# A cross-attention and quantised FFN kernel: one block from the projections to the attention's output, with the maxima of two head groups taken in the projections

## The reference

```
q, k, v = layernorm(x) @ Wq + bq, ctx @ Wk + bk, ctx @ Wv + bv
x = x + softmax(q k^T / sqrt(32), masked) v @ Wo + bo
      # image rows (768) see their own third of the image; text rows (256) see
      # all image tokens and, causally, the text
xn = layernorm(x)
xq = fake_quant(xn)                  # int8 grid, scale from the largest |xn| of all
h  = silu(xq @ Q(w_gate)^T) * (xq @ Q(w_up)^T)      # I = 1408
x = x + fake_quant(h) @ Q(w_down)^T  # Q: int8 grid, one scale per row
```

## Time and profile before

| | |
|---|---|
| three runs | 1151.24, 1147.26, 1150.76 us; median 1150.76 |
| the profiled execution | 1151.39 us, span 1149.6 us, mean granted clock 0.951 |
| busy share of the span | PE 92%, PEld 62%, DVE 66%, ACT 44%, POOL 56% |
| DMA | 223.86 MB, mean 195 GB/s |

### The profile page before, as it was taken

How to read it: one execution, slowest core, us unless ns; L and a number is a source line. 1 busy time by engine, 2 the same in 40 slices (tenths; PEclk the granted TensorE clock), 3 DMA queues, 4 the chain that set the end, 5 groups by cost and what they waited for, 6 DMA issues and landing times. The chain is left out here.

```text
span 1149.6 us, 18244 instructions
## 1 busy us (share of the span) xinstructions
PE 1056.8 (92%) x6550; PEld 707.7 (62%) x6550; DVE 754.6 (66%) x1351; ACT 511.3 (44%) x882; POOL 639.0 (56%) x347
## 2 busy tenths in 40 slices
PE   5999999999629999999999999899986799999898
PEld 4888888888516656656666666457865344444343
DVE  5665456654329667776777777335988487777785
ACT  3322223222102667666776666671111455554553
POOL 3434454344440889998999999754764112100373
PEclk9999999999955999999999999799998799999899
DMA  5987677856699897898999863348996454100876
GB/s 201 322 259 236 218 279 257 270 172 196 208 178 194 172 228 166 196 201 184 205 208 209 200 154 122 98 129 226 327 255 226 119 200 148 36 1 1 326 241 220
DMA packets 134324, 223.86 MB, mean 195 GB/s; under 512 B 29672, under 2 KB 60136, under 8 KB 132778
## 3 DMA queue, kind: packets, MB, share of 16 engines
q1 hardware_dynamic: 134250, 222.89, 70.1%
HBM read 137.65 MB, written 80.62 MB: 190 GB/s over the span
## 5 line engine op out<-in xcount | busy, mean ns | idle before, releaser
L800 ACT ACTIVATE a_probs<-a_banks 128x512 f32<-128x512 f32 (+2 forms) x512 | 233.4, 535 | 135.4 <-PE a_banks L1016 101.4
L733 POOL TENSOR_TENSOR a_pair_sums<-a_probs,a_probs 128x2048 f32<-128x2048 f32 x48 | 221.7, 4620 | 69.8 <-ACT a_probs L800 61.1
L875 DVE TENSOR_REDUCE a_max<-a_banks 128x2 f32<-128x512 f32 x192 | 123.0, 684 | 53.6 <-PE a_banks L987 53.4
L1016 PE MATMUL a_banks<-a_queries,a_keys 97*128 97x512 f32 x384 | 147.6, 428 | 8.4 <-ACT a_probs L800 6.3
L992 PE MATMUL a_banks<-a_keys,a_queries 96*128 96x512 f32 (+1 forms) x256 | 115.1, 463 | 2.7 <-DVE a_max_parts L875 2.7
L987 PE MATMUL a_banks<-a_keys,a_queries 96*128 96x256 f32 x384 | 86.2, 319 | 32.2 <-DMA a_queries<-q_split 32.1
L871 DVE CUSTOM_DVE_ANT_0 a_masked_scores<-a_banks,kept_mask 128x384 f32<-128x384 f32 (+1 forms) x128 | 79.5, 621 | 46.5 <-PE a_banks L992 46.3
L875 DVE TENSOR_REDUCE a_max_parts<-a_banks 128x1 f32<-128x512 f32 x128 | 87.8, 686 | 26.1 <-PE a_banks L992 22.7
L987 PEld LDWEIGHTS a_banks<-a_keys,a_queries 96*128 96x128 f32 x384 | 69.8, 204 | 54.9 <-DMA a_queries<-q_split 32.8
L1389 POOL TENSOR_TENSOR d_out<-d_out,f_x 128x512 f32<-128x512 f32 x28 | 42.6, 1551 | 96.5 <-DVE d_out L1417 96.5
L225 POOL TENSOR_SCALAR p_x<-p_x,p_neg_mean,p_rstd 128x512 f32<-128x512 f32 x32 | 28.1, 889 | 121.6 <-DVE p_rstd L330 121.6
(11 more groups left out here) (173 smaller groups left out, 2208.6 us busy)
## 6 DMA issues: line engine op xcount, KB each, us to landing
a_keys<-k_split SPq DMA_DIRECT2D x48, 512.0 KB, 8.1
a_queries<-q_split SPq DMA_DIRECT2D x48, 512.0 KB, 14.3
f_x<-x_scratch SPq DMA_DIRECT2D x14, 1024.0 KB, 7.8
p_c<-in_ctx_dram SPq DMA_DIRECT2D x8, 1024.0 KB, 8.8
p_x<-in_x_dram SPq DMA_DIRECT2D x8, 1024.0 KB, 11.0
v_scratch<-p_v_stage SPq DMA_DIRECT2D x16, 512.0 KB, 9.1
k_split<-p_stage_hi SPq DMA_DIRECT2D x16, 512.0 KB, 4.2
k_split<-p_stage_lo SPq DMA_DIRECT2D x16, 512.0 KB, 5.3
```

Of the source, the lines that this page charges most:

```text
L733: pool.tensor_tensor(PP[u % 2], PR[2 * c % 4], PR[(2 * c + 1) % 4], ALU.add).then_inc(paired, 1)
L800: act.activation(PR[kt % 4][:, j, 0:w], STB[:, n % NST, 0:w], ACT.Exp, scale=SCALE).then_inc(edone, 1)
L875: dve.tensor_reduce(out, src, AX.X, ALU.max).then_inc(wfree, 1)
L1016: op = pe.matmul(out.rearrange("p (c t) -> p c t", t=SIT), keys, q, start=True, stop=True)
```

## The change

The projections and the attention with its output become one block, and share one set of 8 PSUM banks and the two arenas of SBUF.

- **Banks and buffers of the projections.** Items go round banks 0, 1, 2, 6, 7 (`NB = 5`), the attention's three banks of pieces are apart. Two stage pairs serve k and then q. Context, turned context and turned x have one buffer instead of two. `FR` is a buffer of its own.
- **Order in a step.** On VectorE the layernorm of the next chunk moves from between x and k to among q (`moments` behind its first tile, `deviations` behind its third), and `ffn_rows` from among k to behind q's third and fourth tile (first and second in the last step). SP stores the FFN rows behind the next step's v stores, and loads the next ones behind the first k store.
- **Maxima of groups 0 and 1.** Stack 0 is loaded in steps 4 and 5, stack 1 in steps 5 and 6. The 28 pieces of group 0 are put behind q's tiles of step 5 (2 each), v's and q's of step 6 (4 and 1 each), those of group 1 behind v's and q's of step 7 (4 and 3 each). The turn and shift row of group 0 come in step 7.
- **First groups.** The pieces of groups 2, 3 and 4 are spread over 7 slots each from slot 3 of group 0 on. `TURN_SLOT` is 3. Stack 2 is loaded behind the last q store, shift row 1 ahead of stack 3. The last FFN store lies in group 0, the scales' in group 1.
- **Output stage.** `root(n)` ahead of `hi(n + 2)`, `lo(n + 1)` behind the first tile of `chunk(n)`.

The core of the diff:

```diff
+NB = 5
+EARLY = 4
-TURN_SLOT = 1
+TURN_SLOT = 3
+CATCH_UP, SHORT = 3, 7
...
+        STG = [tuple(mem.over(f"p_stage_{part}{i}", (4 + i) * TILE + h * TILE // 2, [P, 2, CH], F32R)
+                     for h, part in enumerate(("hi", "lo"))) for i in range(2)]
+        PB = (0, 1, 2, 6, 7)
         def bank(u, i):
-            return BK[:, (KT + u * ITEMS + i) % NB, :]
+            return BK[:, PB[(KT + u * ITEMS + i) % NB], :]
...
+            def step(b, u):
+                n = 2 * b + u
+                late = n - EARLY if isinstance(n, int) else None
+                last = not more(n, 1)
...
                 for i in range(2):
+                    A.load_early(sp, late, i)
+                if more(n, 2):
                     s.reach(sp, free, NB + at(n) + XTURN + KT)
                     load_x(n + 2, u)
+                stage_store(n, 0)
+                s.reach(sp, fst, 32 * (n + 1))
+                ffn_load(n, u, b)
+                stage_store(n, 1)
+                A.load_early(sp, late, 2)
...
+                if more(n, 2):
+                    s.reach(sp, free, NB + at(n) + CTURN + KT)
+                    load_c(n + 2)
+                if late == 2:
+                    sp.wait_ge(full, at(n) + CTURN + KT)
+                    for part in range(3):
+                        A.load_stack(sp, 1, part)
+                stage_store(n, 2)
+                A.load_early(sp, late, 3)
+                stage_store(n, 3)
+                if not last:
+                    for i in range(2):
+                        value_store(n + 1, i)
+                        if i == 0 and not more(n, 2):
+                            A.shift_rows(sp, 0)
+                    ffn_store(b, u)
...
             def staged(u, n, i, j, use, bias):
                 if j % 2 == 0:
-                    act.wait_ge(sout[stage + j // 2], 32 * (n + 1))
+                    act.wait_ge(sout[j // 2], 32 * (2 * n + use + 1))
...
                 for j in range(KT):
+                    staged(u, n, query(n) + j, j, 0, (3 if more(n, 1) else 2) * KT + j)
+                    if more(n, 1) and j == 0:
+                        moments(1 - u, n + 2, b + u)
+                    if more(n, 1) and j == 2:
+                        deviations(1 - u, n + 2)
+                    if more(n, 1) and j >= 2:
+                        ffn_rows(n, j - 2)
+                    elif not more(n, 1) and j < 2:
+                        ffn_rows(n, j)
+                    if j == (3 if more(n, 1) else 1):
+                        ffn_rows(n, 2)
+                        ffn_rows(n, 3)
+                    for i, k in A.early(n, KT + j):
+                        A.largest(dve, i, k)
...
+        FIRST = [(n, item) for n, items in ((EARLY + 1, range(KT, 2 * KT)), (EARLY + 2, range(2 * KT)), (EARLY + 3, range(2 * KT)))
+                 for item in items]
+        COUNT = (2,) * 4 + (4,) * 4 + (1,) * 4 + (4,) * 4 + (3,) * 4
...
             for i in range(NGRP):
                 if i == 0:
+                    load_values(sp, 1)
+                    for row in range(6):
+                        load_stack(sp, 2, row)
+                    front.ffn_last(sp)
                 store(i, 0)
                 if i > G and i % G == 1:
                     store_recs(i // G - 1)
+                if i + 1 < NGRP:
+                    shift_rows(sp, i + 1)
                 store(i, 1)
+                if i == 0:
+                    for row in range(6):
+                        load_stack(sp, 3, row)
...
+                if u < 2:
+                    pool.wait_ge(front.sout[u], 32 * (2 * NCH + 1))
...
             for n in range(NCH):
+                root(n)
                 if n + 2 < NCH:
                     hi(n + 2)
-                root(n)
...
                     op = dve.bn_stats(ST[:, t, :], X1[u][:, t, :])
+                    if t == 0 and n and n + 1 < NCH:
+                        lo(n + 1)
...
-                if n + 2 < NCH:
-                    lo(n + 2)
```

More of the change, by code:

```diff
@@ L362, in step @@
                     dve.wait_ge(full, at(n) + VALUE + t + 1)
-                    dve.tensor_tensor(VST[t // 2][:, t % 2, :], bank(u, VALUE + t), BV[:], ALU.add).then_inc(free, 1)
+                    dve.tensor_tensor(VST[t // 2][:, t % 2, :], bank(u, VALUE + t), BV, ALU.add).then_inc(free, 1)
+                    for i, k in A.early(n, t):
+                        A.largest(dve, i, k)
+                    if t == 0 and not more(n, 1):
+                        A.rows_out(dve, 0)
                 for j in range(KT):
-                    turned(XT[u], u, n, XTURN + j, j)
@@ L381, in _ @@
             weight(0, "v")
-            layernorm(0, 1, 0)
+            moments(0, 1, 0)
+            deviations(0, 1)
             weight(1, "k")
@@ new lines, in load_early, with sync @@
+        def load_early(sp, late, place):
+            part = 4 * late + place if late is not None else 9
+            if part < 6:
+                load_stack(sp, 0, part)
+            elif part < 9:
+                load_stack(sp, 1, part - 3)
+        A.load_early = load_early
+        A.load_stack, A.load_values, A.shift_rows, A.ones_row, A.early = load_stack, load_values, shift_rows, ones_row, early
+        A.wfree, A.pieces, A.reduced, A.masked = wfree, 0, 0, 0
+        def sync(sp, front):
@@ L1029, in values @@
                     pe.wait_ge(ifree, 3 * i + kt // 2)
+                if kt == 0 and i == 0:
+                    for bank in (6, 7):
+                        pe.wait_ge(front.free, front.cleared(bank))
                 if kt == 0:
@@ L1112, in _ @@
                 pe.wait_ge(olo, m + 1)
[L1113 removed]
+                chunk(m)
+        A.tensor = tensor
+        return A
 class Scale:
```

661 lines of the change are left out of this document (351 added, 310 removed).

## The result

The changed kernel takes **1191.3 us** (median of 4 runs, 1188.4 to 1197.9), the kernel before beside it 1149.0 (1146.7 to 1151.2): ratio 1.039, 95% interval 1.036 to 1.043. It is 42 us slower. The forecast was 1134 with a range that ended at 1152; even the slower rival (B, 1159) is 32 us short of it.

What follows compares the result with a forecast made beforehand. Projections were held bound by TensorE, the attention by GpSimd, so its chain's start counts. Pair sums 10 us earlier, first groups 2 us lost, output stage 9 gained: -17 us, 1134 us; eight in ten 1117 to 1152.

Steps and rivals of the forecast that it cites:

- B: Rival: the ring reaches TensorE in every projection step, rounds over 40 us, half clock after long stalls; 1159 us, chance 0.10.
- The ring: Projections: q's staging waits for k's store behind FFN load, FFN store and quantising; round 37.4 to 39 us, 14 us reach TensorE.
- The 7 us of slack: Projections: the ring can fall back about 7 us before it reaches TensorE, as the norm is wanted at the next x turns.
- Pieces: Projections, steps 5 to 7: maxima of groups 0 and 1 add 15 us of TensorE and 17.5 us of VectorE's backlog.
- Seam at the end of the projections: GpSimd's first pair sum starts 7.8 us after the projections' end, at 361.2, 10 us earlier than before.
- Groups 0 to 3: First attention groups: late stack 2 and group 2's shift row cost 2 us (0 to 6), GpSimd's slack taking most.
- Output stage: With the root first, VectorE's wait goes and chunks take 12.5 us; 9 us gained, range 2 to 11.
- A: Rival: the DMA queue keeps up in the projections and the ring's 14 us vanish; 1120 us, chance 0.22.
- C: Rival: the output stage stays with the DMA queue, 7 us more than forecast; 1141 us, chance 0.13.
- D: Rival: the shift row is late in each steady attention group, about 10 us in all; 1144 us, chance 0.10.

Runs made afterwards that it cites:

- experiment 4: Changed kernel with the maxima of groups 0 and 1 behind the projections, block and early stack rows as changed: 1190.4 us.
- experiment 12: 11 without the edit of (10), with that of experiment 4, and stack 3 behind group 0's shift row: 1123.6 us, ratio 0.981 to the kernel before.
- kernel of 8: Experiment 3's kernel with x ahead of FFN store, that between late v stores, early stack rows behind q's stores, stack 4 behind a shift row: 1157.5 us.
- (10): Kernel of 8 with the pieces of the maxima put behind k tiles instead of q tiles: 1150.5 us.
- Experiment 3: Changed kernel with the norm's deviations and both FFN row maxima at q's second tile instead of its third and fourth: 1165.8 us.
- experiment 6: Kernel of Experiment 3 with each step's x load issued ahead of the FFN store instead of behind it: 1159.4 us.
- experiment 2: Changed kernel with the next context load moved from behind k's second store to behind q's last one: 1193.0 us.
- experiment 1: Kernel before with only the change's output stage (root ahead of hi(n+2), lo(n+1) inside chunk n): 1143.1 us, ratio 0.996.
- 11: Kernel of 8 with the edits of experiment 9 and (10), without that of experiments 5, stack 3 directly behind the first output store: 1146.1 us, ratio 0.997.
- experiments 5: Changed kernel with the six rows of stack 4 issued behind group 2's shift row instead of ahead of it: 1192.1 us.
- experiment 9: Changed kernel with the shift rows of groups 1 to 15 issued on ScalarE's queue instead of SP's: 1181.6 us.

## Why the prediction was wrong

The end of the projections in five kernels separates the two causes:

| last projection matmul done at | maxima behind | maxima inside |
|---|---|---|
| transfers ordered as in the change | 351.0 (4) | 388.5 (the change) |
| ring opened | 309.0 (12) | 351.2 (8), 341.8 (10) |

The numbers in brackets are those of the experiments. "Opened" means the transfers reordered and the row maxima at q's second tile. The kernel before ends the projections at 306.8. So the ring costs 37 us with the pieces inside and 42 without them, and the pieces 37.5 us with the ring and 33 to 42 without it: the two add up to within 5 us. By way of (4), 42.0 for the ring, 37.5 for the pieces and the 2.2 between 306.8 and 309.0 make the 81.7.

**The ring: right mechanism, the step that failed is its size.** The prediction named it (k store, FFN load, FFN store, quantising) and put a round at 37.4 to 39 us; it is 42.3 to 43.6. The part on the engines was right: from the landing of k's second store to the FFN store 21.3 us measured, 0.95 + 2.2 + 0.7 + 1.9 + 13.6 + 1.6 = 21.0 foreseen. The DMA part was 16 to 17, and is 21.7 (77.36 to 99.09): FFN store, x, two k pairs and FFN load, issued within 8 us, are 4.8 MB, and in this burst they move at 4.8/21.7, some 220 GB/s (the queue's whole rate in this stretch is 263, with what is issued behind them), where I gave the 1 MB transfers 380. The prediction wrote that B decides from a round of 40 us and is worth 28 us; it took 14 as the "middle of 0 and 21". At 42 to 43 us it is 6 a step in steps 2 and 3, and 10 in step 4, where the first stack rows go out: 24 us at the x turn of step 5 (236.48 less 211.60, of which 0.9 is the start), and with the steps behind it 42 to 44 in all (experiment 4). Experiment 3 shows it by moving one link, experiment 6 by taking 1 MB out, experiment 2 that the load behind has no part in it. The 7 us of slack held for one step and a half.

**The clock behind a wait: put at nothing.** The forecast counted waits, and only rival B spoke of half clock. Counted in the timelines up to the end of the projections, 82 of the 1110 512-column projection matmuls of the changed kernel start 0.43 us apart instead of 0.23 or lie between the two, 58 in experiment 4, 52 in the kernel of 8, and 15 before the change as in experiment 12. The time added is some 8 us of the ring's 42 (experiment 4 against 12) and 6 to 7 of the pieces' cost. TensorE's waits are another 28 us of the ring's 42; the remaining 6 were not traced.

**Pieces: the sum was short.** 32.5 us forecast (15 of TensorE, 17.5 of waits); 37.5 measured with the changed order, 42.2 with the ring opened. The sum of the waits is right, by luck: TensorE waits 17.3 us for reductions in the kernel of 8, 11.2 behind q tiles, where 6.6 were foreseen, and 6.1 behind v tiles, where 10.2 were. Behind a q tile VectorE, from which TensorE wants a piece bank back, is itself waiting, in order, for the low part of the tile and so for a k store's landing; I had walked VectorE's own work and left out what it waits for. The trace of before could not show it, since no such pair stood there. What was missing in the sum are 1.6 us of waits for stack rows (6.6 in the changed kernel) and the slow matmuls behind the waits: 15 + 17.3 + 1.6 + 6.7 are 40.6 of the 42.2. The 15 are the forecast's own estimate and were not measured apart. With pieces at k tiles the 32.8 us look like the forecast's, but they hold 7.8 of waits for rows.

**Seam at the end of the projections: right.** The first pair sum was put 7.8 us behind the end; it is 7.7 (388.5 to 396.1), by quantising.

**Groups 0 to 3: wrong by 19 us.** Forecast +2 (0 to 6), measured +21.5 (from +24.9 to +46.4), the second largest miss. Both waits were named: stack 2 landed 24 us behind the end (21 foreseen) and cost 5.6 us at slot 3; the shift row of group 2 was "wanted 5 us before it lands" and cost 13.4: SP, held for 11.4 us by one store, issued it 8 us late, and it took 10.5 us to land between the stacks. I took issues as free. "GpSimd's slack takes most" was a hope; GpSimd has hardly any gap in a steady group. Before, stacks 0 and 1 were issued ahead of the first scores and stack 2 at 356.6, 15 us ahead of the first pair sum; stacks 3 and 4 followed at 380 and 390; the change issues stack 2 at 392, 4 us ahead of it, and 3 and 4 back to back from 419 to 433.

**Output stage: right, smaller.** Forecast 9 (range 2 to 11); 5.7 by the trace, 4.4 (1.7 to 7.0) by the timed comparison. The wait for the root is gone as foreseen; the term that failed is 12.5 us a chunk to the end, since the last two chunks take 15.0 and 14.5 (experiment 1).

**Rivals.** A (the queue keeps up) is refuted: ScalarE waits for k's stores in each of steps 1 to 6. C gave the output stage 2 us and the forecast 9; the 4.4 to 5.7 measured lie between them. D is refuted: the landing's median fell to 3.0 us. B is what happened (steps 2 and 3 take TensorE 42 us), and the time is 32 us above its price; the largest parts are 14 to 16 us in the ring (42 to 44 instead of 28), 15 in the first groups and 5 in the pieces. The chance of slower, 0.10, was far too low: ring, stacks and shift row leaned on one queue, and I added them as if they were independent.

**What the change itself is worth.** Its output stage, the one block and the early stacks, with the shift rows on ScalarE's queue, bring 22 us together once the ring is opened and the maxima stand behind the projections (experiment 12), 4 to 6 of them from the output stage. Its idea of taking maxima inside a stage bound by TensorE brings nothing in these orders: the 33.6 us that it removes come back as 33 to 42, and at the first pair sum the kernel with the maxima inside is level (the change against 4) or 8.7 us behind (11 against 12). The other 14 us by which 11 is slower than 12 can't be laid on the maxima alone, since stack 3 stands elsewhere too. Open is how much of the 22 us belongs to the block, to the early stacks and to the shift rows' queue; this was not separated.

## What to carry to other kernels

When work is moved in one queue, draw the ring that it closes (who waits for which landing, and what that releases) and price its transfers as one burst, not one by one: here the same transfers were put at 16 to 17 us and took 21.7, so a round that comes within some per cent of the stage's step may well be the bound. Filling a stage whose one engine is always busy with small pieces that need a bank back from a second engine costs what the pieces cost plus everything that the second engine waits for, and the slow clock behind each long wait; a stretch bound by another engine that can cover loads, as the 38 us here, may be worth keeping. And a repair that only shifts a jam shows by the same wait, with the same size, one period later.

## What was not expected of the hardware

- The issue of a DMA is not always cheap: while two stacks (6 MB) were under way at about 200 GB/s, single small stores (128 KB) held SP for 11.4, 11.1 and 11.9 us (the changed kernel, experiments 5 and 9); the same store otherwise takes mostly 0.3 to 0.6 us. What sets this length was not tried.
- A 16 KB row on another engine's queue landed in 2.2 us in the median and in 9.2 us while stacks were moving (experiment 9).
- In experiment 1 a VectorE operation on 128x4 values took 4.56 us once (at 785.69), and two others on such values 3.1 and 2.6 us, where most take 0.2; the cause is not seen in the trace.
